# A residual chain of four conditioned layers: on the sync queue, the moves of the activations go ahead of the stores of the block diagonals

## The reference

```python
# L0: gated MLP, F = 1376, with adapters of rank 16 (A, B picked by itok_B_2_6)
gate = x @ W_gate.T + 0.5 * (x @ A_gate[i].T) @ B_gate[i].T
up   = x @ W_up.T   + 0.5 * (x @ A_up[i].T) @ B_up[i].T
act  = silu(gate) * up
x    = x + act @ W_down.T + 0.5 * (act @ A_down[i].T) @ B_down[i].T
# L1: a 32 x 32 matrix per batch (picked by itok_B_0_15) mixes the 32 rows
x    = x + einsum('bct,bcd->bdt', x, W1[cond])
# L2: x @ W.T plus the best two of 8 low-rank experts, logits biased by itok_B_0_7
x    = x + l2(x)
# L3: as L1, with other matrices
x    = x + einsum('bct,bcd->bdt', x, W3[cond])
```

## Time and profile before

| | |
|---|---|
| three runs, us | 579.43, 580.84, 581.45 |
| the profiled execution, us | 578.02, of it span 576.2 |
| TensorE busy (PE) | 554.8 us, 96% |
| VectorE (DVE), ScalarE (ACT), GpSimd (POOL) busy | 55%, 35%, 37% |
| mean granted TensorE clock | 0.994 |
| DMA of SyncE's queue | 60.00 MB, 31.1% of the 16 engines' span |

### The profile page before, as it was taken

How to read it: one execution, slowest core, us unless ns; L and a number is a source line. 1 busy time by engine, 2 the same in 40 slices (tenths; PEclk the granted TensorE clock), 3 DMA queues, 4 the chain that set the end, 5 groups by cost and what they waited for, 6 DMA issues and landing times.

```text
span 576.2 us, 8757 instructions
## 1 busy us (share of the span) xinstructions
PE 554.8 (96%) x3224; PEld 500.7 (87%) x3224; DVE 319.4 (55%) x734; ACT 202.8 (35%) x400; POOL 215.7 (37%) x229
## 2 busy tenths in 40 slices
PE   5999999997989898999999999999999999999997
PEld 5889988896979797888989989898989899999995
DVE  5797344543444443535454554545454467777876
ACT  6774223333232333232323232324233433333330
POOL 5752045654463737151323222222321032443430
PEclk9999999998999999999999999999999999999999
DMA  8973355566474747465556455554555721234321
GB/s 301 357 260 126 110 180 171 190 193 183 156 231 148 225 150 212 147 195 185 172 166 183 150 175 171 154 185 147 179 156 182 282 86 56 74 130 144 110 93 73
DMA packets 62666, 97.83 MB, mean 170 GB/s; under 512 B 8352, under 2 KB 32032, under 8 KB 62624
## 3 DMA queue, kind: packets, MB, share of 16 engines
q1 hardware_dynamic: 51600, 60.00, 31.1%
q0 software_dynamic: 10880, 37.23, 20.8%
q10 hardware_dynamic: 144, 0.04, 0.0%
HBM read 74.44 MB, written 22.81 MB: 169 GB/s over the span
## 4 chain that ended last, share of the span: by engine, by line
PE 72%; DMA 9%; DVE 6%; POOL 5%; issue 3%; SPq 2%; ACT 2%; DVEq 0%; ACTq 0%
PE gu_ps L1268 10%; PE gu_ps L1270 10%; PE gu_ps L1269 9%; PE down_ps L1268 7%; PE down_ps L1269 7%; PE down_ps L1270 6%; DMA x_res<-act_blocks 5%; PE l_ps L1268 5%; PE l_ps L1269 5%; PE l_ps L1270 5%; POOL a_raw L746 3%; DMA act_blocks<-act 3%; PE gu_ps L1276 2%; PE gu_ps L1275 2%; SPq L675 1%
## 5 line engine op out<-in xcount | busy, mean ns | idle before, releaser
L1268 PE MATMUL down_ps<-wd_sb,act_hl 128*128 128x288 f32 (+1 forms) x352 | 107.1, 304 | 11.1 <-DVE act_hl L1031 10.9
L746 POOL DMA_INDIRECT b_sel_raw<-b_gu,idx_rank x48 | 48.7, 1014 | 176.7 <-PE gu_ps L1276 166.1
L1269 PE MATMUL down_ps<-wd_sb,act_hl 128*128 128x288 f32 (+1 forms) x352 | 105.0, 298 | 0.0
L1270 PE MATMUL down_ps<-wd_sb,act_hl 128*128 128x288 f32 (+1 forms) x352 | 104.9, 298 | 0.0
L1268 PE MATMUL gu_ps<-w_sb,xt 128*128 128x512 f32 x256 | 102.1, 399 | 0.0
L1270 PE MATMUL gu_ps<-w_sb,xt 128*128 128x512 f32 x256 | 100.3, 392 | 0.0
L1269 PE MATMUL gu_ps<-w_sb,xt 128*128 128x512 f32 x256 | 100.2, 391 | 0.0
L746 POOL DMA_INDIRECT a_raw<-a_all,idx_batch x60 | 64.8, 1080 | 60.1 <-DVE wd_sb L1031 46.1
L1268 PEld LDWEIGHTS down_ps<-wd_sb,act_hl 128*128 128x128 f32 (+1 forms) x352 | 67.4, 191 | 15.3 <-DVE act_hl L1031 13.7
L1095 DVE TENSOR_TENSOR act<-act,gu_ps 128x512 f32<-128x512 f32 (+1 forms) x47 | 29.8, 633 | 88.6 <-ACT act L864 88.5
L864 ACT ACTIVATE act<-gu_ps 128x512 f32<-128x512 f32 (+1 forms) x47 | 26.1, 555 | 133.3 <-PE gu_ps L1276 133.3
(11 more groups left out here) (154 smaller groups left out, 1066.6 us busy)
## 6 DMA issues: line engine op xcount, KB each, us to landing
act_blocks<-act SPq DMA_DIRECT2D x39, 256.0 KB, 2.9
x_res<-act_blocks SPq DMA_DIRECT2D x156, 64.0 KB
xt_raw<-x_t SPq DMA_DIRECT2D x16, 256.0 KB, 4.9
w_sb_raw<-wgu SPq DMA_DIRECT2D x16, 256.0 KB, 8.4
x_res<-x_rows SPq DMA_DIRECT2D x16, 256.0 KB, 2.7
x_after_l<-x_res SPq DMA_DIRECT2D x16, 256.0 KB, 2.0
bd<-bd_hl SPq DMA_DIRECT2D x16, 256.0 KB, 2.1
x<-x_after_l SPq DMA_DIRECT2D x16, 256.0 KB, 2.7
```

Of the source, the lines that this page charges most:

```text
L746: nc.gpsimd.indirect_dma_start(out=dst, out_offset=None, in_=table, in_offset=bass.IndirectOffsetOnAxis(ap=idx, axis=0)).then_inc(s, 16)
L1268: pe.matmul(out_, stationary[0], moving[0], start=start, stop=False, skip_group_check=True)
L1269: pe.matmul(out_, stationary[0], moving[1], start=False, stop=False, skip_group_check=True)
L1270: return pe.matmul(out_, stationary[1], moving[0], start=False, stop=stop, skip_group_check=True)
```

## The change

In steps 10 to 25 `store_bd(s - 10)` goes behind `move_act(s - 1)` on the sync queue. In step 7 `store_tile(1)`, which stood ahead of `move_act(6)`, goes into it, between the store of the activations and their reading back, whose buffer it has to empty first.

```diff
@@ move_act(d): after the store of act_blk (line 668)
                 if d - 1 in MOVED:
                     sp.wait_ge(s_lo, s_lo_of(("act", d - 1)))
                 else:
+                    store_tile(1)
                     sp.wait_ge(s_xout[1], 16)
                 sp.wait_ge(s_aout, 16 * moved(d))
@@ the loop over the steps
-                if 0 <= s - W13_FIRST - 2 < NT:
-                    store_bd(s - W13_FIRST - 2)
                 if s == STEPS - 3:
...
-                if s == step_of(2, 1):
-                    store_tile(1)
                 if s - 1 in MOVED:
                     move_act(s - 1)
+                if 0 <= s - W13_FIRST - 2 < NT:
+                    store_bd(s - W13_FIRST - 2)
                 if s >= FREE:
```

## The result

The changed kernel takes 563.56 us (median of four runs, 562.91 to 563.71), the kernel before 580.14 (the three runs shown above and one beside the changed kernel, 579.43 to 581.45). The ratio is 0.971, interval 0.969 to 0.973: 16.6 us less. In a later comparison it was 569.75 against 584.69, ratio 0.976, interval 0.972 to 0.981: 14.9 less. The forecast was 565.3 within 561.5 to 572.0. Medians in this document are over all runs of a kernel; ratios and their intervals use only the runs within 1.5% of its fastest.

The account below looks back on a forecast made before the run. TensorE bounds the kernel, losing time where it idles or runs slowly behind held act stores. Gains of 13.7 + 0.4 = 14.1 us, plus 1.4 of the median's excess, take 580.84 to 565.3, range 561.5 to 572.0.

Parts of the forecast that it names:

- The 13.7 of the five tiles: Tiles from 115.11 to 266.46: loss against 27.53 us per tile, 10.2 TensorE idle plus 3.5 slow clock, all regained.
- The clock went with the idle time: TensorE in the five tiles: 3.5 us of slow clock follow from its idle time and vanish with it.
- First step: Of a tile, counted from the finished tile's store: act store at +3.6 instead of +11.0, loads at +7.9, block at +13.7.
- Third step: Of a tile: loads +24.8 to +26.5, block diagonal's store until +26.8, finished tile's store at +27.5, 0.7 us to spare.
- the first rival: Half cured: act store amid GpSimd's gathers lands late, so the act block comes late; 570 us, chance 0.13.
- At most 0.8 lost, the landing is at most 3.6: ScalarE's cast after a tile's first step waits at most 0.8 us for the block diagonal's store; slack of 2.8 covers it.
- the slower rival: ScalarE gets stuck behind the later block diagonal store in each of five tiles; about 585 us, chance 0.04.
- listed under "right": Five tiles: act store within 0.1 us of transpose, no act_hl waits, periods 27.5 to 27.7, clock 1.00, line 656 waits stand.
- listed under "wrong": Five tiles: TensorE waits for act_hl or td_hl, loads later than +9, ScalarE idle over 3 us, low clock without idle.
- Step 7: store_tile(1) within move_act: gain 0.7 us at best, loss up to 3.3, taken as 0.4 gain.
- Half of the 2.82 us: Median of runs above the profiled execution: half taken as curable slow clock after long waits, 1.4 us.
- the cured case: All five long TensorE waits go: 565.3 us, spanning 562.0 to 568.5, chance 0.80.

Follow-up runs that it names:

- again: The kernel before, run once more with no edit; median 585.04 us of twelve runs, the profiled one 586.06.
- the first hold of 8: Changed kernel plus 8 small DMAs of 512 bytes ahead of the act store in the first step of the five tiles; 572.23 us.
- the hold of 24: Changed kernel plus 24 small DMAs of 512 bytes ahead of the act store in the first step of the five tiles; 587.56 us, ratio 1.006.
- the hold of 8 again: Changed kernel with the same 8 small DMAs ahead of the act store, run a second time; 573.85 us, ratio 0.980.
- the last experiment: Changed kernel with each block diagonal's store one step later, behind that step's act store and ahead of its loads; 618.9 us, ratio 1.049 to the kernel before.

## Why the prediction was right

**The cause and its size.** Right: the mechanism held, and the forecast gain was off by about 1 us. The hold of the act store by the block diagonal was the loss: taking it away in three ways (behind the move, between its halves, by GpSimd) gives the same rest of 448.5 to 448.9 us, and putting a hold of that length back gives 470.3. The forecast's gain for the profiled execution was 14.1; from profile to profile it was 15.1, and the rest fell by 14.2. How near the median of 563.56 came to 565.3 is in part luck: the five tiles gave 14.4 and not 13.7, the start ended 0.9 earlier in the second profile, and in the later comparisons, with a later start, the same kernel took 569.75 and the one with the block diagonals alone 568.89.

**The 13.7 of the five tiles** was 1.0 too small, and it was the anchor. I counted from the store of a tile, and the one at 115.11 was itself 1.0 late, for VectorE's add had ended at 113.43 + 0.69 = 114.12. From add to add:

```profile
113.43:265.75 152.32, 142.10 (x787) 0.98 0.57 181
265.75:430.93 165.18, 165.18 (x944) 1.00 0.54 170
```

152.32 - 5 x 27.53 = 14.7. After, the same five tiles took 250.43 - 112.51 = 137.92 by the same adds: 14.4 gained, the floor of 137.65 all but reached. Of these, 10.2 are the five waits, and 3.5 are busy time in the two tiles with a clock of 0.95, as forecast. The other 0.7 is busy time in the three tiles at full clock (27.8 us each against 27.6), a term that the prediction lacks and whose cause is open.

**The clock went with the idle time.** Right in all traces. A stretch of the tile at 206 before, and two of the tiles after:

```profile
229.00:231.00 2.00, 2.00 (x10) 0.50 0.62 189
```

```profile
112.51:140.17 27.66, 27.66 (x159) 1.00 0.65 202
140.17:167.68 27.51, 27.51 (x159) 1.00 0.67 205
```

In five traces with waits here (before, again, the tile's store alone, the first hold of 8, the hold of 24) the clock fell to its half for 3 to 7 us with all seven idle stretches of 2.7 to 3.7 us, with two of nine of 2.3 to 2.6, and with none of six of 0.8 to 1.9. In the hold of 8 again it did not fall with its one of 2.44, and in the last experiment it fell with eight of ten of 2.9 to 5.1, not with those of 2.87 and 3.09. So the length of the idle stretch alone does not decide it. It never fell in these tiles without one. That agrees with the Trainium skill (TensorE: Matmul & The Clock Gate, Part 1), by which activity releases the throttled clock.

**The queue, step by step.** First step: "the act store goes at +3.6" was true in two tiles; in the others it went at +5.6, +4.8 and +4.1. The block diagonal's store did not wait for GpSimd "as before", but was behind the loads and found its data ready (58.7 us of waits to 0.8). Third step: "0.7 to spare" is the point that failed. The end of the tile whose add is at 140.17:

```profile
131.57 2.88 SPq L676 DMA_DIRECT2D x_res<-act_blocks  x4
134.49 0.43 SPq L656 DMA_DIRECT2D bd<-bd_hl  x1
134.96 0.43 SPq L668 DMA_DIRECT2D act_blocks<-act  x1
140.04 1.74 SPq L676 DMA_DIRECT2D x_res<-act_blocks  x4
...
142.31 0.43 SPq L621 DMA_DIRECT2D x_after_l<-x_res  x1
...
138.37 0.41 ACT L940 CAST bd_hl<-bd_raw 128x256 fp32r<-128x256 f32 x1 [4.72 <-DMA bd<-bd_hl]
...
139.39 0.63 DVE L1030 TENSOR_TENSOR act_hl<-x_res,act_hl 128x384 fp32r<-128x384 f32 x1
```

The loads wait for VectorE's split of the block before, and that stood behind ScalarE's wait for the block diagonal: the split ended at 140.02, and the loads went at 140.04 (+26.8, where I had +24.8). The block diagonal followed, and the finished tile's store went at 142.31, 1.45 us after its data were ready, and then the residual, x and the next act store in turn. So ScalarE's wait in one tile is what held the next tile's act store, at +4.8. It cost nothing, for the slack of 2.8 took it.

In the other tiles the third step's act store took 3.2 to 4.2 us to land, where those of the six later tiles took 2.3 to 3.8 before. Over all act stores, then over those of the block diagonals, in the changed kernel, against 2.9 and 2.1 as medians in the earlier trace rows:

```profile
DMA to landing us min/median/max: 2.2/4.0/6.0
...
DMA to landing us min/median/max: 2.2/2.2/4.4
```

The longer landing of the act stores fits the Trainium skill's rule that stands beside the first rival (DMA: Bandwidth & Descriptors, Queues, rings and completion order), for these stores now go while gathers are under way; no run took the gathers away, so that is not shown. The rival itself did not come true; nothing was half cured.

**ScalarE.** "At most 0.8 lost, the landing is at most 3.6" was wrong by much: after the first step it lost up to 1.6 us, and after the second it waited up to 4.7, where I had it hidden. The median landing of the block diagonals hardly changed (2.2). In the tile of the 4.7 two things add up: the store was issued at +21.3 and not +19.6, for the loads ahead of it went late and took 2.88 us to issue, and it landed in 3.8. In the changed kernel that is still hidden, with the block ready at +17.2 at the latest (+17.4 in its second trace). The margin is 1.5 us (1.3) and not the 2 to 3 that I had. The mechanism of the slower rival was the right one to fear, and its price was too low: it decides earlier, and it goes round.

**The signs.** No wait for `act_hl` was left in the five tiles, the periods were 27.5 to 27.7 us and the clock 1.00, as listed under "right". But the act store followed the transpose within 0.1 us in two of the five tiles only, and the queue's waits at line 656 did not stand. Two of the signs listed under "wrong" did appear: the loads went later than +9 in three tiles (+10.8, +10.0, +10.1), and ScalarE stood over 3 us at its cast (4.7). The slack hid both; the signs had been set tighter than the slack.

**Step 7**: the 0.4 us taken for it is not shown. The waits went from 0.7 to 0.3 us between the first two traces, but were 1.3 in the second trace of the changed kernel, and alone it changed the time by 0.1, within the interval.

**Half of the 2.82 us.** The median fell by 16.6 where 15.5 was forecast. The rest of the kernel before was 462.8, 464.1 and 465.0 in three traces, so its runs do lose up to 2.2 more there than in the first profile, in the traces with the longer waits; against 448.6 that is a gain of 14.2 to 16.4. The other part of what a run has above the profile is the start. Which of the two the four runs of the first comparison had cannot be told, for only one of them has a trace. The 562.0 given as the lower end of the cured case is not a sum of its terms, which give 563.6.

## What to carry to other kernels

A store that nobody is waiting for can still be the costliest instruction of a queue, if the data it waits for come late and something urgent is behind it: order a queue by when each item can go and by who needs it. But follow the release of that store's buffer as well as its issue, for a store that falls into a burst of another queue's transfers lands late (6.3 us here, where 2.1 is usual), and a wait in a loop with one buffer comes back every turn. Measure from an event that the change cannot shift.

## What the runs showed of the hardware

The store of a block diagonal, 256 KB on the sync queue, landed in 2.1 us as a median where it went ahead of the act store, and in 2.2 right behind the four loads. Where GpSimd's gathers came in between it took 6.3 us until ScalarE was let go (hold of 8), and right behind the act store 4.8 (the last experiment, 127.12 to 131.96). A small DMA of 512 bytes took 0.25 us to issue as a median, and 24 of them 7.39 us (from 182.84 in the third of the five tiles of the hold of 24).

The third tile's end lay at 112.5 to 120.4 us in the thirteen traces, though the kernels differ before it only in step 7 and in the place of the first block diagonal's store. It goes with the clock at TensorE's first transposes: the three traces in which the clock did not fall there end the tile at 112.5 to 115.0 us, three in which it was at its half for 3 to 4 us at 115.4 to 117.1, and seven with about 7 us of it at 118.1 to 120.4. In seven of these ten late ones TensorE waited 1.4 to 5.6 us for VectorE's first mask. Two traces taken on the same chip, of the holds of 8 and 24, end it at 117.1 and 115.0, so it is not the chip alone. What decides it is open.
